# Linear attention stage: the next batch's rows normed at the end of VectorE's step, and turned and copied behind the batch's last products

## What is computed

```
def _L1_attn_ref(x, Wq, Wkv, Wproj, bproj):      # x = _layernorm(h), h: (8, 1056, 64), 8 heads of 8
    q = einsum('bnc,oc->bno', x, Wq)             # split in heads
    k, v = einsum('bnc,oc->bno', x, Wkv)         # the same
    q = elu(q) + 1
    k = elu(k) + 1
    k_sum = k.sum(axis=2)
    D_inv = 1 / maximum(einsum('bhnd,bhd->bhn', q, k_sum), 1e-6)
    context = einsum('bhnd,bhne->bhde', k, v)
    attn = einsum('bhnd,bhde->bhne', q, context) * D_inv
    out = attn (heads side by side) @ Wproj.T + bproj
```

## Time and profile before

| | us |
|---|---|
| median of 3 runs | 2579.44 (2574.83 to 2582.92) |
| the profiled execution's own time | 2577.83 |
| its span | 2575.8 |
| the stage's first `kneg` to its last | 1586.43 to 1682.32 |

### The profile page before, as it was taken

One profiled execution on the slowest core, in us unless ns is written; L12 is line 12 of the kernel. 1 busy time (PEld: TensorE's weight loads), 2 busy tenths in 40 slices (PEclk: granted clock), 3 DMA queues, 4 the chain that ended last, 5 costly groups with the idle time before them and its releaser, 6 DMA issues.

```text
span 2575.8 us, 55956 instructions
## 1 busy us (share of the span) xinstructions
PE 2295.5 (89%) x20539; PEld 1061.5 (41%) x20570; DVE 1828.7 (71%) x4716; ACT 1414.1 (55%) x2560; POOL 424.8 (16%) x502
## 2 busy tenths in 40 slices
PE   8987679999999999999689996687799999699998
PEld 3326523333333333333534443575544444533333
DVE  4566768888888888885367775559767775366765
ACT  2116727777777777777045553327566667144443
POOL 2002200000000000000622433132100100411110
PEclk9996769999999999999589998756699999589999
DMA  3113620101101011030755553255612222734422
GB/s 96 25 31 102 211 75 26 39 26 29 37 26 39 26 30 35 26 65 6 159 147 150 154 149 74 67 118 158 236 45 67 72 91 43 161 76 100 97 61 61
DMA packets 254594, 208.35 MB, mean 81 GB/s; under 512 B 191747, under 2 KB 198132, under 8 KB 254068
## 3 DMA queue, kind: packets, MB, share of 16 engines
q1 hardware_dynamic: 241154, 176.50, 25.9%
q0 software_dynamic: 10368, 19.06, 2.6%
q10 hardware_dynamic: 2808, 9.22, 1.5%
HBM read 138.85 MB, written 65.90 MB: 79 GB/s over the span
## 4 chain that ended last, share of the span: by engine, by line
PE 74%; DVE 10%; ACT 5%; issue 4%; POOL 3%; DMA 2%; SPq 1%; DVEq 0%; ACTq 0%; POOLq 0%
PE ps L1580 11%; PE ps L1486 7%; PE ps L1551 6%; PE ps L2813 3%; PE ps L2293 3%; PE ps L2800 3%; PE ps L2309 3%; PE ps L1191 3%; PE ps L1165 3%; PE ps L2824 3%; PE ps L364 3%; PE ps L1576 3%; PE ps L376 2%; PE ps L1103 2%; PE ps L1106 1%
## 5 line engine op out<-in xcount | busy, mean ns | idle before, releaser
L1666 DVE TENSOR_REDUCE att_mpart<-ps 128x1 f32<-128x512 f32 x1024 | 633.8, 684 | 55.4 <-PE ps L1486 50.3
L1624 ACT ACTIVATE att_p<-ps 128x704 f32<-128x704 f32 x768 | 546.4, 760 | 214.6 <-PE ps L1551 206.8
L1580 PE MATMUL ps<-att_p,att_v 128*9 128x352 f32 x3072 | 300.7, 462 | 0.1
L1486 PE MATMUL ps<-att_kT,att_qT 64*128 64x512 bf16 x1024 | 281.1, 386 | 21.1 <-DMA att_qz<-qt_d 8.4
L1551 PE MATMUL ps<-att_qT,att_kT 64*128 64x352 bf16 x1536 | 251.2, 316 | 7.3 <-ACT att_p L1624 6.9
L1280 DVE TENSOR_REDUCE cau_mpart<-ps 128x1 f32<-128x512 f32 (+5 forms) x384 | 193.2, 552 | 81.1 <-PE ps L1106 67.9
L1247 ACT ACTIVATE cau_p<-ps 128x704 f32<-128x704 f32 (+6 forms) x272 | 171.5, 660 | 82.4 <-PE ps L1165 49.8
L1457 POOL DMA_DIRECT2D o_d<-att_o x128 | 64.3, 509 | 840.2 <-ACT att_o L1607 839.9
L1551 PEld LDWEIGHTS ps<-att_qT,att_kT 64*128 64x128 bf16 x1536 | 82.0, 93 | 272.9 <-issue 263.4
L2367 ACT ACTIVATE mo_g<-ps 128x768 f32<-128x768 f32 x176 | 133.2, 807 | 106.3 <-PE ps L2293 106.3
L2881 ACT ACTIVATE mo_act<-ps 128x512 f32<-128x512 f32 (+1 forms) x216 | 109.7, 559 | 144.8 <-PE ps L2800 144.6
(11 more groups left out here) (414 smaller groups left out, 3828.7 us busy)
## 6 DMA issues: line engine op xcount, KB each, us to landing
mo_gate<-wg_d SPq DMA_DIRECT2D x176, 192.0 KB, 4.0
mo_gate<-wg_d SPq DMA_DIRECT2D x64, 256.0 KB, 5.3
qt_d<-pre_qT SPq DMA_DIRECT2D x8, 1056.0 KB, 4.3
kt_d<-pre_kT SPq DMA_DIRECT2D x8, 1056.0 KB, 7.1
att_kT<-kt_d SPq DMA_DIRECT2D x32, 264.0 KB, 2.7
att_qT<-qt_d SPq DMA_DIRECT2D x32, 264.0 KB, 3.0
cqt_d<-cpr_qT SPq DMA_DIRECT2D x8, 1056.0 KB, 4.4
cau_qT<-cqt_d SPq DMA_DIRECT2D x16, 528.0 KB, 4.0
```

What stands on the lines that cost most here:

```text
L1486: mm = pe.matmul(ps[:, bank, :], qT[half(s), u, j * P:(j + 1) * P], kT[half(s), u, c * BANK:(c + 1) * BANK], start=True, stop=not near)
L1580: mm = pe.matmul(ps[32 * cg:32 * cg + DV, 7, 0:TH], v[:, u, i, s, :], p[:, r, s, :], start=i < 2, stop=i == FULL - 1)
L1624: e = act.activation(p[:, n % PRING, :, :], ps[:, bank:bank + 2, 0:TH], ACT.Exp)
L1666: red = dve.tensor_reduce(mpart[:, j, s, c:c + 1], ps[:, bank, :], AX.X, ALU.max)
```

## The change

Three pieces are moved, each to the end of its engine's step. No instruction is added or taken away, and the orders of POOL and SP stay as they are.

```
@@ PE: step
                 mm.then_inc(S["cx_mm"], 1)
-                if not last:
-                    turn(b + 1)
                 pe.wait_ge(S["cb_made"], b * 2 + 2)
                 for j in range(2):
                     pe.wait_ge(S["qf_made"], b * 2 + (2 if j else 1))
...
                     mm.then_inc(S["o_mm"], 1)
+                if not last:
+                    turn(b + 1)
@@ ACT: step
-                if not last:
-                    copy_turned(b + 1)
                 at_least(act, S["stored"], b * 16)
                 for j in range(2):
                     act.wait_ge(S["o_mm"], b * 2 + j + 1)
...
                         .then_inc(S["o_cp"], 1)
+                if not last:
+                    copy_turned(b + 1)
@@ DVE: step
                     dve.tensor_scalar(kneg[0:n, t0:t1, :], k, 0.0, None, ALU.min).then_inc(S["kneg_made"], 1)
-                if not last:
-                    norm(dve, b + 1, 1 - par)
                 at_least(dve, S["cx_mm"], b)
...
                 dve.tensor_tensor(cb[:, :, D], ps[:, 6, C:C + 1].broadcast_to([P, H]), block_of[:, :, D], ALU.mult)\
                     .then_inc(S["cb_made"], 1)
+                if not last:
+                    norm(dve, b + 1, 1 - par)
```

## The result

The changed kernel takes 2545.4 us (median of 4 runs, 2543.79 to 2547.42) against 2578.51 for the kernel before: a ratio of 0.9872, interval 0.986 to 0.9884, 33.1 us less. The forecast was 2553.0 with a range from 2546 to 2566. What this execution shows of the clock is rival B, in which it never falls behind the first step. Its own time is 2546.72, with a span of 2544.9.

The account below looks back on a forecast made before the run. Bound: a chain of waits round each batch, with the norm ahead of `kf` waiting for `rstd` behind a store. Steps of 11.90 + 4 × 9.09 + 2 × 11.52 = 71.3 replace 95.89, 24.6 less: 2553 us, range 2546 to 2566.

Parts of the forecast that it names:

- rival B: PE's clock never falls behind the stage's first step: stage 66.4 us, 29.4 gained, 2548 us in all; chance 0.20.
- The norm's place and `rstd`: Norm (2.10) and its wait for `rstd` leave the place ahead of `kf`: 3.57 us less per step.
- Outputs ahead, turning last: PE makes outputs (1.11) before turning; k and v start 2.66 behind turning's start, ACT's copy exposed; step 9.09 us.
- The norm beside POOL's work: DVE's norm at its new place meets no POOL work: taken as 0, up to 1.0 us a step if slowed.
- DVE's own round: DVE's measuring behind the norm ends 8.5 us after `kneg` starts, hidden by 0.6 us before the next `kneg`.
- SP's load: Load of batch b+2 has 9 us until use, 16 before; it lands in 2.8 and costs nothing.
- rival C: Next batch's rows come late, so every step waits at DVE ahead of `kneg`: 2586 us or more; chance 0.03.
- rival D: Change doesn't pay: norm still waits, exposed copy and idle time eat the rest; 2572 to 2580 us; chance 0.07.
- The clock: PE's clock falls to 0.50 at the outputs in two of six later steps, at 2.43 us each.
- Rival A: PE's clock stays low in the whole stage: 12.6 to 5.0 us gained, 2565 to 2573 us; chance 0.15.
- The sum: First `kneg` to last: 11.90 + 4 × 9.09 + 2 × 11.52 = 71.3 us in place of 95.89.

Follow-up runs that it names:

- norm and `rstd`: Kernel before with the norm at the end of DVE's step and `rstd` ahead of the store on POOL, turning still ahead of the outputs: 2552.88 us, ratio 0.9911.
- the norm ahead of `cb`: Changed kernel with the norm moved between `qf` and `cb` on DVE: 2574.48 us, ratio to the kernel before 0.9991.
- the repeat: The kernel before run once more with no change, for a second trace: 2576.94 us, ratio 1.000.

## What of the prediction was right, and which step failed

*The norm's place and `rstd`:* right. `kf` comes at T+1.31, the outputs at T+4.23, and `xn` has no wait. What was not seen is that these overlap as causes: moving the norm alone gives 24.7 us of the stage's 29.5, moving `rstd` alone 20.5, and neither adds to the other much. Both shorten the same idle time of PE.

*Outputs ahead, turning last:* the sizes were right: 4.23 + 1.11 + 2.66 + 1.09 = 9.09 forecast, 9.13 measured. What the part is good for was not seen: at equal clock it costs 0.4 a step (9.13 against 8.73), and it pays by the clock, which falls in 2 of 18 later steps with it, in 4 of 6 with the norm alone and in 6 of 6 with norm and `rstd` without it. It cuts PE's idle time of 1.21 behind the context into two shorter ones that stand apart; that this is why the clock holds is argued, not shown.

*The norm beside POOL's work, DVE's own round, SP's load:* all hidden as forecast. The norm takes 2.09; rival C (late rows) and rival D (a wait for `rstd`) didn't occur.

*The clock:* this is the step that failed. The prediction took a fall in two of six later steps at 2.43 each, 4.86 us, from the last batch of the kernel before. The execution has none, and over three executions it is 2 of 18, at 1.6 each. The price was fair as an upper one, as the norm ahead of `cb` shows (2.4); the count was wrong. It rested on one row of one execution, and the repeat shows that row at full clock (1.11 in place of 1.82, above), behind a step with the same long idle time. A second trace of the kernel before would have weakened the ground for the count. What lets the clock fall there in some executions and not in others is open. Rival A, the clock low throughout, didn't occur: the turning by `eye` ran at 1.00, 2.20 us. By that row the rule of the Trainium skill ("TensorE: Matmul & The Clock Gate", "Part 4: PE-mode transpose"), that the full clock doesn't engage for transposes in that mode, doesn't cover these products.

*The sum:* 71.3 forecast, 66.43 measured; of the 4.87 between them the clock is 4.86, the first step 0.25 (11.65 for 11.90) and the sixfold 0.04 takes 0.24 back.

*The rest* of the distance to the measured time lies outside the stage, where the prediction put nothing. Between the two profiled executions the part from the last turning product of the projection `cpj` to the end is 2.6 us shorter (349.8 and 347.2), and the stage starts 1.0 later. With only one of the two, this part or the 4.86 us of the clock, the time would have been inside the range (2550.3 or 2548.0 by these sizes). Over two executions of before and three of the changed kernel the stage differs by 30.1 and the span by 32.2; the end part has 349.8 and 348.7 against 347.2, 347.3 and 347.1. It also has 349.7 with PE's and ACT's part alone and with the norm alone, and 347.3 with the norm ahead of `cb`. So it isn't tied to the order of this stage. The traces show what it goes with. The same stretch, from 38 to 44 us behind the start of that product, before and after:

```profile
2264.00:2270.00 6.00, 6.00 (x29) 2.78 (x33) 3.10 (x25) 1.17 (x3) 0.00 (x0) 0.50 0.73 153
```

```profile
2235.70:2241.70 6.00, 5.40 (x52) 2.41 (x55) 4.76 (x29) 3.70 (x6) 0.00 (x0) 1.00 0.85 167
```

In this stretch PE's clock is 0.50 to 0.55 in the four executions whose end takes 348.7 or more, and 1.00 in the nine others, which have 347.1 to 347.9. Why it comes back later in those four is open; this part of the gain is luck as far as the prediction goes.

## What to carry to other kernels

Work for the next batch belongs behind the last thing that this batch's chain needs, and a helper queue that feeds it (here POOL's `rstd`) belongs ahead of stores that wait for this batch's end. Price PE's idle time in two parts, the wait and the clock that it costs: with the norm ahead of `cb` the second (2.4 us) was as large as the first (2.1). Don't take a count of such falls from one row of one execution; take a second trace of the kernel before. Here the order with the shorter pieces of idle time won, though its step at equal clock is longer (9.13 against 8.73).

## What the runs showed that was not expected

- Filling PE's idle time with useless products made kernels faster: 10.5 us with 14 products a step (2563.98 against 2574.48, from two groups), and 10.0 with four (2542.88 against 2552.88).
- Equal idle time per step didn't mean an equal clock. The changed kernel has 0.88 + 0.93 + 0.46 us idle in a step and mostly kept 1.00; the order with the turning ahead of the outputs has 0.88 + 1.21 and fell in 10 of 12 later steps. That the length of the single piece decides is argued from this pair and from the filled runs, and no run varied it alone.
- POOL's first store came over 3 us late in every trace, shown as "issue" (1603.40 in the earlier trace rows, 1598.36 and 1597.14 above). The cause is open; it costs time only where `rstd` stands behind it (a step of 12.66 us against 10.3).
